# Mamba block: project stage stores each part once, the scan stage makes the copies, two casts move to ScalarE, B and C come from one product

## The reference, cut to what matters

```python
xi, z = jnp.split(xn @ W_in, 2, axis=-1)                 # 512 + 512 columns
u = silu(causal_conv4(xi, conv_w) + conv_b)              # 4 taps, per channel
x_dbl = u @ W_xproj                                      # 16 + 64 + 64 columns
dt_r, Bm, Cm = x_dbl[..., :16], x_dbl[..., 16:80], x_dbl[..., 80:]
delta = softplus(dt_r @ W_dt + b_dt)
def step(h, (d_t, B_t, C_t, u_t)):                       # over 2048 tokens
    h = h * exp(d_t[:, :, None] * A) + (d_t * u_t)[:, :, None] * B_t[:, None, :]
    return h, einsum('bdn,bn->bd', h, C_t)
y = (ys + u * D) * silu(z);  out = residual + y @ W_out
```

## Time and profile before

| | |
|---|---|
| time, median of 3 runs | 5863.85 us (5862.06 to 5864.1) |
| profiled execution: its own time | 5866.2 us |
| its span (first to last instruction) | 5864.4 us |
| VectorE busy | 5532.8 us, 94% |
| TensorE busy | 5246.8 us, 89% |
| ScalarE busy | 3525.5 us, 60% |
| DMA | 547.19 MB, 93 GB/s over the span |

### The profile page before, as it was taken

The page is one execution under the profiler, slowest core; times in us unless marked ns, Lnnn a source line. Parts: engine busy times, 40 slices in busy tenths (PEclk is TensorE's granted clock), DMA queues, the critical chain, the costliest instruction groups (busy, mean ns, idle before and its releaser), DMA issues. The chain is left out here.

```text
span 5864.4 us, 150087 instructions
## 1 busy us (share of the span) xinstructions
PE 5246.8 (89%) x38780; PEld 2480.8 (42%) x38780; DVE 5532.8 (94%) x3683; ACT 3525.5 (60%) x8302; POOL 2302.3 (39%) x6767
## 2 busy tenths in 40 slices
PE   2999959999999999999999999999999999997999
PEld 1444324444444444444444444444444444445666
DVE  5799989999999999999999999999999999995776
ACT  6777746666666666666666666666666666662333
POOL 4000024444454444444444444444444444440111
PEclk7999979999999999999999999999999999998999
DMA  4899962222222222222222222222222222224342
GB/s 156 298 334 334 340 197 53 53 54 55 55 52 53 54 55 55 52 54 54 55 54 51 55 54 55 54 52 54 55 54 53 52 54 55 54 45 142 118 137 74
DMA packets 1105510, 547.19 MB, mean 93 GB/s; under 512 B 753744, under 2 KB 1015056, under 8 KB 1105056
## 3 DMA queue, kind: packets, MB, share of 16 engines
q1 hardware_dynamic: 1093776, 533.89, 33.8%
q10 hardware_dynamic: 11664, 12.52, 0.6%
HBM read 296.83 MB, written 249.82 MB: 93 GB/s over the span
## 5 line engine op out<-in xcount | busy, mean ns | idle before, releaser
L988 DVE TENSOR_TENSOR_SCAN s_h<-s_decay,s_ubank 128x1024 f32<-128x1024 f32 x2048 | 4461.0, 2261 | 13.5 <-ACT s_ubank L953 13.3
L940 ACT ACTIVATE s_decay<-s_abank 128x512 f32<-128x512 f32 x4096 | 2210.3, 595 | 2.2 <-PE s_abank L878 1.1
L863 PE MATMUL s_ybank<-s_h,s_window 128*8 128x256 f32 x16416 | 1948.3, 602 | 1.9 <-DVE s_h L988 1.9
L904 PE MATMUL s_ubank<-s_x,s_w 128*128 128x256 bf16 x8192 | 1246.3, 275 | 371.2 <-DVE s_h L988 370.8
L1024 POOL TENSOR_TENSOR s_carry<-s_decay,s_h 128x64 f32<-128x64 f32 x2032 | 884.2, 435 | 1750.4 <-ACT s_decay L940 1577.2
L953 ACT ACTIVATE s_ubank<-s_seed 128x64 f32<-128x64 f32 x2048 | 478.2, 233 | 1710.3 <-PE s_ubank L904 1326.8
L878 PE MATMUL s_abank<-xnT,s_a 128*128 128x256 bf16 x8192 | 1257.0, 274 | 33.0 <-DMA s_w<-scratch_b_rows 29.9
L904 PEld LDWEIGHTS s_ubank<-s_x,s_w 128*128 128x128 bf16 x8192 | 675.8, 98 | 1193.4 <-DVE s_h L988 1091.7
L878 PEld LDWEIGHTS s_abank<-xnT,s_a 128*128 128x128 bf16 x8192 | 758.4, 98 | 197.7 <-ACT s_decay L940 40.2
L863 PEld LDWEIGHTS s_ybank<-s_h,s_window 128*8 128x8 f32 x16416 | 377.9, 97 | 838.8 <-issue 729.8
L1028 POOL TENSOR_TENSOR s_seed<-s_carry,s_first 128x64 f32<-128x64 f32 x2048 | 660.2, 322 | 164.3 <-ACT s_first L946 3.9
(11 more groups left out here) (129 smaller groups left out, 3194.1 us busy)
## 6 DMA issues: line engine op xcount, KB each, us to landing
s_x<-scratch_u_rows SPq DMA_DIRECT2D x4096, 32.0 KB
scratch_u_rows<-p_u_turn SPq DMA_DIRECT2D x90, 1024.0 KB, 6.7
scratch_delta_rows<-p_dparts SPq DMA_DIRECT2D x136, 512.0 KB, 6.2
xnT<-scratch_delta_rows SPq DMA_DIRECT2D x1024, 64.0 KB, 2.7
scratch_y<-s_y SPq DMA_DIRECT2D x1036, 16.0 KB
scratch_sz<-p_sz SPq DMA_DIRECT2D x16, 1024.0 KB, 6.2
scratch_u<-p_u SPq DMA_DIRECT2D x16, 1024.0 KB, 7.9
s_w<-scratch_b_rows SPq DMA_DIRECT2D x256, 64.0 KB, 2.4
```

What stands on the lines that cost most here:

```text
L863: last = nc.tensor.matmul(y_bank[32 * ct:32 * ct + WIN, 1 - x, :], window[:, of, (at + t) * WIN:(at + t + 1) * WIN], H[:, 1 - x, :, t], st ...
L904: last = nc.tensor.matmul(dst.rearrange("p q (a t) -> p a q t", t=2), w2[:, g, 4 * s + 2 * x + e, :], x2[:, s, :, 2 * x + e, q:q + 32, :], ...
L940: nc.scalar.activation(dst.rearrange("p x q t -> p q x t"), a_bank[:, b].rearrange("p j r (x t) -> p (j r) x t", x=2), ACT.Exp).then_inc(e ...
L988: nc.vector.tensor_tensor_scan(H[:, x, PT * p:PT * p + PT, :].rearrange("p q t -> p (q t)"), decay[:, x * (1 + c % 2), p].rearrange("p q t ...
```

## The change

- Delta's and du's parts are stored once each (three DMAs of 512 KB and three of 1 MB a tile). The other places, five of `delta_rows` and two of `u_rows`, are filled by DMAs from DRAM to DRAM (`copy_rows`, seven a tile). SyncE issues those of tile 0 late in the project stage and those of tile i+1 in the scan of tile i, one after each even chunk from chunk 0 to chunk 12 of its 16. SyncE's scan loop now has 16 chunks as its body, with the last 16 written out behind it.
- The casts of line 691 leave VectorE. ScalarE makes them (`second_delta` before Abs, `second_u` between Abs and Exp), for the tile split one step before. On VectorE the last parts move: delta's behind du's remainder, du's (`split_last`) behind `split_b`.
- `w_x` holds B and C once. One product of 128 rows gives B in rows 0 to 63 and C in rows 64 to 127, one ScalarE copy reads it (`bc_in`), `split_b` splits all 128 rows, and C is stored to DRAM twice from its 64 rows. The second product (four matmuls) and the copy of line 605 go.
- VectorE clears two more tiles at the start, and ScalarE waits for the clearing.

```diff
-COPIES = (2, 2, 1, 1)
+COPIES = (1, 1, 1, 1)
-        w_x = sb("p_w_x", [P, MI, RANK + 4 * NS])
+        w_x = sb("p_w_x", [P, MI, RANK + 2 * NS])
...
             def back_stores(i, c, b):
+                sp.wait_ge(d2_done, i + 1)
                 sp.wait_ge(d3_done, i + 1)
-                for k, (_, j) in reversed(list(enumerate(COMBOS))):
+                for k, (_, j) in reversed(list(enumerate(COMBOS[:3]))):
...
-                        if j == part and k < PLACES:
+                        if j == part and k < 3:
...
-                    sp.dma_start(d["C"][:, rows], c_out[:, :]).then_inc(c_stored, 16)
+                    for h in range(2):
+                        sp.dma_start(d["C"][h * NS:h * NS + NS, rows], bc_in[NS:P, :]).then_inc(c_stored, 16)
...
                 back_stores(i, c, b)
+                if isinstance(b, int) and c == 0:
+                    sp.wait_ge(dparts_stored, 16 * 3 * (i - 1))
+                    for j in range(3):
+                        sp.wait_ge(turns_stored[j], 16 * COPIES[j] * (i - 1))
+                    for n in range(N_COPIES):
+                        copy_rows(sp, d, 0, n, copied)
...
                 rows(0, RANK, 2 * NS)
-                rows(1, RANK + 2 * NS, 2 * NS)
...
+            def second_delta(i):
+                act.wait_ge(dr_done, i + 1)
+                nc.scalar.activation(dparts[:, 1], w1[:, :, :], ACT.Identity).then_inc(d2_done, 1)
+
+            def second_u(i):
+                act.wait_ge(ur_done, i + 1)
+                nc.scalar.activation(uparts[:, 1], du[:, :, :], ACT.Identity).then_inc(u2_done, 1)
...
+                second_delta(i)
+                act.wait_ge(back_read, i * 6 + 11)
                 nc.scalar.activation(ex[:, :, :], v[:, :, :], ACT.Abs).then_inc(abs_done, 1)
+                second_u(i)
                 act.wait_ge(abs_done, i + 1)
                 nc.scalar.activation(ex[:, :, :], ex[:, :, :], ACT.Exp, scale=-1.0).then_inc(exp_done, 1)
...
-                nc.scalar.activation(c_out[:, :], bk_bank[:, 1, :], ACT.Identity).then_inc(back_read, 1)
+                act.wait_ge(c_stored, i * 32 + 32)
+                nc.scalar.activation(bc_in[:, :], bk_bank[:, 0, :], ACT.Identity).then_inc(back_read, 1)
...
+                nc.vector.tensor_copy(dparts[:, 0], lw[:, :, :]).then_inc(d1_done, 1)
+                nc.vector.tensor_tensor(w1[:, :, :], lw[:, :, :], dparts[:, 0], ALU.subtract).then_inc(dr_done, 1)
...
+                nc.vector.tensor_copy(uparts[:, 0], du[:, :, :]).then_inc(u1_done, 1)
+                dve.wait_ge(u1_done, i + 1)
+                nc.vector.tensor_tensor(du[:, :, :], du[:, :, :], uparts[:, 0], ALU.subtract).then_inc(ur_done, 1)
+                dve.wait_ge(d2_done, i + 2)
+                nc.vector.tensor_tensor(dparts[:, 2], w1[:, :, :], dparts[:, 1], ALU.subtract).then_inc(d3_done, 1)
...
+            def split_last(i):
+                dve.wait_ge(u2_done, i + 3)
+                nc.vector.tensor_tensor(uparts[:, 2], du[:, :, :], uparts[:, 1], ALU.subtract).then_inc(u3_done, 1)
...
+N_COPIES = NCB - 3 + PLACES - 3
+def copy_rows(eng, d, i, n, done):
+    if n < NCB - 3:
+        cols = bass.ds(i * TW + TW, TW)
+        eng.dma_start(d["delta_rows"][3 + n][:, cols], d["delta_rows"][n % 3][:, cols]).then_inc(done, 16)
+    else:
+        k = n - (NCB - 3)
+        rows = bass.ds(i * TW + 2 * TW, TW)
+        eng.dma_start(d["u_rows"][rows, 3 + k, :], d["u_rows"][rows, k, :]).then_inc(done, 16)
...
-            over_chunks(sp, chunk)
+            def tile(i, more):
+                sp.wait_ge(copied, i * (16 * N_COPIES) + 16 * N_COPIES)
+                for k in range(per):
+                    chunk(i * (per // 4) + k // 4, i * per + k, k % 4)
+                    if more and k % 2 == 0 and k // 2 < N_COPIES:
+                        copy_rows(sp, d, i + 1, k // 2, copied)
```

More of the change, by code:

```diff
@@ L402, in project_stage @@
         turns_stored = [sem(f"turns_stored{j}") for j in range(4)]
-        n_weights = 10
+        copied = sem("p_copied")
+        n_weights = 6
         block = ctx.enter_context(nc.Block())
@@ L426, in _ @@
             sp.dma_start(w_in[:, :, :], d["W_in"].rearrange("(k p) n -> p k n", p=P)).then_inc(weights, 16)
-            sp.dma_start(w_x[:, :, 0:RANK], wx[:, :, 0:RANK]).then_inc(weights, 16)
-            for r in range(4):
-                at, frm = RANK + NS * r, RANK + NS * (r // 2)
-                sp.dma_start(w_x[:, :, at:at + NS], wx[:, :, frm:frm + NS]).then_inc(weights, 16)
+            sp.dma_start(w_x[:, :, :], wx[:, :, :]).then_inc(weights, 16)
             sp.dma_start(w_dt[:, :], d["W_dt"]).then_inc(weights, 16)
@@ L557, in _ @@
             act.sem_inc(turn_read, 11)
+            act.sem_inc(u2_done, 1)
             act.wait_ge(weights, 16 * n_weights)
@@ L622, in take_turn @@
                                              ACT.Identity).then_inc(turn_read, 1)
+            act.wait_ge(cleared, 4)
             for m in range(8):
@@ L630, in _ @@
                     take_turn(i, g)
+                if i == NT:
+                    second_delta(NT)
+                    second_u(NT)
         @block.vector
@@ L637, in _ @@
             nc.vector.memset(dparts[:, :, :, :], 0.0).then_inc(cleared, 1)
-            nc.vector.memset(c_out[:, :], 0.0).then_inc(cleared, 1)
+            nc.vector.memset(bc_in[:, :], 0.0).then_inc(cleared, 1)
             nc.vector.memset(xi[:, :, 0:TAPS - 1], 0.0).then_inc(xi_free, 1)
@@ L680, in split @@
             def split(i):
-                for src, rest, parts, free, first, whole, one, left, two, three, had in (
-                        (lw, w1, dparts, (dparts_stored, i * (16 * NCB) + 16 * NCB), delta_done, i + 2, d1_done, dr_done,
-                         d2_done, d3_done, 1),
-                        (du, du, uparts, (turned, i * 8 + 16), du_done, i + 3, u1_done, ur_done, u2_done, u3_done, 2)):
-                    dve.wait_ge(first, whole)
-                    dve.wait_ge(*free)
-                    nc.vector.tensor_copy(parts[:, 0], src[:, :, :]).then_inc(one, 1)
-                    dve.wait_ge(one, i + 1)
-                    nc.vector.tensor_tensor(rest[:, :, :], src[:, :, :], parts[:, 0], ALU.subtract).then_inc(left, 1)
-                    dve.wait_ge(left, i + 1)
-                    nc.vector.tensor_copy(parts[:, 1], rest[:, :, :]).then_inc(two, 1)
-                    dve.wait_ge(two, i + 1)
-                    nc.vector.tensor_tensor(parts[:, 2], rest[:, :, :], parts[:, 1], ALU.subtract).then_inc(three, 1)
+                dve.wait_ge(delta_done, i + 2)
@@ new lines, in split @@
+                dve.wait_ge(dparts_stored, i * 48 + 48)
+                nc.vector.tensor_copy(dparts[:, 0], lw[:, :, :]).then_inc(d1_done, 1)
+                dve.wait_ge(d1_done, i + 1)
+                nc.vector.tensor_tensor(w1[:, :, :], lw[:, :, :], dparts[:, 0], ALU.subtract).then_inc(dr_done, 1)
+                dve.wait_ge(du_done, i + 3)
+                dve.wait_ge(turned, i * 8 + 16)
+                nc.vector.tensor_copy(uparts[:, 0], du[:, :, :]).then_inc(u1_done, 1)
+                dve.wait_ge(u1_done, i + 1)
@@ L713, in step @@
                 split_b(i)
+                split_last(i)
             front(0, 0, 0)
@@ L837, in chunk @@
                 store_y(f, c % 2, f * 2 + 1)
-            over_chunks(sp, chunk)
+            per = NF // NT
+            def tile(i, more):
[4 more added lines that the diff above has]
+                        copy_rows(sp, d, i + 1, k // 2, copied)
+            with sp.Fori(0, NT - 1) as i:
+                tile(i, True)
+            tile(NT - 1, False)
             for f in range(NF, NF + 3):
```

35 lines of the change are left out of this document (18 added, 17 removed).

## The result

The changed kernel takes 5900.83 us (median of 4 runs, 5900.14 to 5904.74) against 5863.29 us of the kernel before beside it (4 runs): ratio 1.0066, 95% interval 1.005 to 1.0082. I had forecast 5874 us and a range that ended at 5892. The span of the profiled execution is 5899.1 us, 34.7 more than that of before, and the two traces split this into three stretches.

The account below looks back on a forecast made before the run. VectorE was taken as the project stage's bound before the change. Loop +15.8, start +3.9 and -1.0, last step +2.9, tail -2.4, drain -9.5 gave +9.7 us on 5863.85: 5874 us rounded, range 5848 to 5892.

Parts of the forecast that it names:

- the scan "as long as now": Scan stage: its length in the profile after would equal that of the kernel before, adding 0 us.
- The copies: Seven DRAM-to-DRAM copies a tile on SyncE: their issue is hidden by its 6.07 us average wait; taken as 0.
- the copies collide: Scan: large copies delay the loads and VectorE stands still; 2 us for each of 30, +60 us, 5934; chance 0.08.
- the clock: Project loop: TensorE waits 4 to 6 us before each third front product, falls to half clock, adding 1.67 us a tile.
- The rival without the fall: Project loop: TensorE's clock doesn't fall; 36.3 us a tile, sum -10.5 us, 5853; also called the second rival; chance 0.18.
- My first chain: Project loop: dependences through ScalarE from one tile's third front product round to the next tile's; 36.07 us without the fall.
- The 5.93: Project tile, first chain: average time from dt rows read to the end of `v`, 5.93 us.
- The 5.16 + 3.86: Project tile, first chain: end of `v` to end of Exp, 5.16 us, plus two ScalarE casts, 3.86 us.
- Start: Before line 666 of tile 0: casts delay it 3.86 us; fewer weight DMAs against two more clearings give -1.0.
- Last step: Project stage, tile 14 to 15, without convolution: +3.86 - 0.48 - 0.5 = +2.9 us.
- VectorE's tail: Project stage after the last step, where VectorE alone leads: two casts less, -2.4 us.
- Drain: Last part of B to scan start: fewer stores, 17 us in place of 26.5, -9.5 us (bounds -6 and -12).

Follow-up runs that it names:

- run 16: The changed kernel with 32 idle instructions on SyncE ahead of its scan loop of 16 chunks: 5887.31 us, ratio 1.0041.
- run 1: The kernel before with only SyncE's scan loop changed to 16 chunks as its body, the last 16 written out, no copies: 5901.56 us, ratio 1.0067.
- run 3: Changed kernel with SyncE's scan loop of 4 chunks, quartered copies, and TensorE's waits for the last u and B parts moved to the fifth transposes: 6038.61 us.
- run 13: run 9 with both casts back on VectorE: 5849.58 us, ratio 0.9977.
- run 9: kernel 7 with 32 idle instructions on SyncE in the project stage, ahead of the scan loop: 5849.89 us, ratio 0.9979.
- runs 9 to 12: In order, 32, 64 and 96 idle instructions ahead of kernel 7's loop, then 64 in the kernel before: 5849.89, 5849.38, 6055.68 and 6141.42 us.
- run 12: The kernel before with 64 idle instructions on SyncE in the project stage, scan loop unchanged: 6141.42 us, ratio 1.0475.
- run 5: The kernel before with eight idle instructions behind each chunk of SyncE's scan loop of 4 chunks: 6081.76 us, ratio 1.0376.
- kernel 7: The changed kernel with three copies per 4 chunks issued from ScalarE's queue and SyncE's scan loop back to 4 chunks: 6028.46 us, ratio 1.0282.

## Why the prediction was wrong

**The step that failed most: the scan "as long as now".** Under "The copies" I priced the seven copies of a tile and took 0. That price was nearly right: 3.3 us (runs 16 and 1). But the change had also turned SyncE's loop of 4 chunks into one of 16, which I described and gave no price at all. Of the 52.1 us that the forecast lacks, 35.8 come with that loop alone (run 1) and 12.9 with the place where it lies (run 16). A scan in which VectorE is busy for 4460.9 of 4465 us has nothing to hide 3 us of SyncE in, when the loads have 1.7 us in hand. The rival "the copies collide" forecast a longer scan (+60 us) by another mechanism, and its evidence (stalls behind large copies) isn't in the trace.

**The second: the clock.** I put one wait of 4 to 6 us, and 1.67 us for it, into every tile. The size was right where the fall meets the third front product: from there to the dt rows it is 18.55 to 18.58 us in the three tiles where it does, and 18.55 in the tile shown of run 3, in place of 16.88. The condition wasn't. The split of u ends later (`split_last` stands last), and the first group of transposes waits for it, so TensorE's idle time is cut in two, or stands before the second front product. I had followed only the wait for ScalarE's reads, and not the queue of TensorE in front of it. In six tiles no front product is slow; in the five where the second is, the dt rows come only 0.1 to 0.2 us later than in these. The Trainium skill (TensorE: Matmul & The Clock Gate, "HAM oscillation — how this bites in real kernels") has bursts with waits between them fall back to half clock in every round. By that rule, run 3 agrees, with a slow product in all 14 tiles. The changed kernel shows bursts with waits between them too, and there the trace has the fall in eight tiles of 14.

**The third: the tile under it.** The rival without the fall has 36.3 us a tile, and 36.32 was measured over the loop. That is luck. The tiles without any slow product take 34.98 to 35.05 us. My first chain holds there: in the tile that ends at 611.80 it is 16.88 to the dt rows, 5.25 to the end of `v`, 8.61 to the end of Exp, 1.31, 2.30 and 0.64, together 34.99. Two terms were too long. The 5.93 for the dt rows to the end of `v` is a mean over tiles with a fast and a slow `W_dt` product (3.88 to 5.67 us in the kernel before, where ScalarE's wait before Ln took up the difference). The 5.16 + 3.86 counted ScalarE's passes at 1.93 us, and one behind another they start 1.80 apart (416.77, 418.57, 420.37). Against this stand the two tiles behind a turn of the loop, 39.88 and 39.24 where 37.6 would have followed. An estimate from these tiles: 508.44 - 14 x 34.98 - 2 x 1.42 (the later start of the third front product behind a turn) leaves some 16 us of the loop to slow products. In run 13, with the casts back on VectorE, the tiles stand 36.4 us apart, and in run 9 without that edit 36.5, the fast ones 35.0: what the move gives in the fast tiles it loses in the slow ones and behind the turns.

**What the rest of the sum gave.** Without the clock the forecast for the stage was -10.5 us, the second rival, and -14.2 was measured; its premise, a clock that doesn't fall, isn't met.

- Start: 3.86 - 1.0 = +2.9 forecast, +3.3 measured (205.43 against 202.16).
- Loop: 510.8 forecast without the fall and 531.0 with it, 508.44 measured. That VectorE would wait for ScalarE and Ln wouldn't was right.
- Last step: +2.9 forecast; +1.2 measured, 713.87 to 741.93 against before's 717.38 to 744.24.
- VectorE's tail: -2.4 forecast; -2.8 measured.
- Drain: 17 us forecast, 17.4 measured, by chance. I had reckoned with stores; VectorE's clearing of `xnT` ends it (3.36 + 13.71 + 0.28). In the kernel before the same clearing ends at 788.26 and the scan starts at 797.64, so there something else ended last, and the fewer stores fit that. The gain stops where the clearing takes over.

**What stays open.** That the place of SyncE's loop decides is shown by runs 9 to 12. That the time goes into bringing in instructions is argued from the packets, which come with the stall in every kernel and never without it; no trace shows which instruction waited for which packet. The bounds (298 and 554) are those of these programs, and 278 us for the shifted kernel before against 220 for the padded one is explained only in part: SyncE's gap at a turn is 4.80 to 4.94 us in run 12 and 3.45 to 3.70 in run 5 (the turns from 1000 to 1500 us), VectorE idles 57.5 us more over the same number of turns, and why the gap is longer is open. What decides in a tile of the project loop whether TensorE's clock falls isn't shown either.

## What to carry to other kernels

When a change rewrites a loop, price the loop and not only the work put into it: look at what the engine's queue does between the last instruction of one round and the first of the next, and at how much the loads behind it have in hand. If the instruction queue of the page moves many packets in a kernel with loops, try a few idle instructions ahead of the loop: 32 of them were worth 180 us in kernel 7. The same trial can cost: 64 of them ahead of the loop of the kernel before cost 278 us. And follow each engine's queue in order before giving a wait a length: a second wait in front of it can cut it in two. Read such a wait in every round of the trace and not in one: the tile shown first here is one of six, and the other eight are different.

## What the runs showed of the hardware

- At a turn of the scan loop SyncE's last DMA and the next are 0.74 to 0.86 us apart where the turn is free (kernel before, runs 9 and 10), 3.0 to 3.7 in the changed kernel and runs 1, 5, 7 and 16, and 4.8 to 4.9 in run 12, by where the loop lies in the engine's stream of instructions. Loops of 219 to 227 built instructions were free when they began at 298 or later and ended by 554; the same loop of 219 moved by 32 instructions made 5849.9 us into 6028.5.
- A free turn moves no instruction packets to speak of (44 or 45 in the whole run); a dear one moves 5 of 8 KB, and in the loops of 16 chunks 13 to 14.
- TensorE's granted clock, of its two levels the full one, stayed at 1.00 through two waits of 1.48 and 1.26 us with work between them, and fell to 0.52 behind one of 3.88 (run 3). Behind a wait of 2.46 us it fell to 0.50 in one tile of the changed kernel (277.21) and stayed at 1.00 in another (242.24).
- ScalarE's passes of 128x2048 f32, shown 1.90 us long, start 1.80 us apart when one stands behind another (416.77, 418.57, 420.37).
- A DRAM-to-DRAM copy of 512 KB landed 4.1 us after its issue and one of 1 MB 5.6 us (medians of 80 and 32, changed kernel).
